# A graph layer with routed experts: sums added straight into the output, and the gate's logits taken from the node products

## What is computed

```python
xn = layernorm(x)
# graph part: gate of every edge, message, sum by target node, update
gate = sigmoid(silu(edge @ W1 + b1) @ W2 + b2)
aggr = segment_sum(gate * xn[src], dst)
upd  = silu(concat([xn, aggr]) @ U1 + c1) @ U2 + c2
# linear attention: kv = k^T v / N with layer-normed k and v; mix = (q @ kv) @ wo.T + bo
x = x + xn + upd + mix
# routed experts on the normed rows
xn2    = layernorm(x)
logits = xn2 @ gate_w + gate_b
top-2 softmax weights p; out = x + sum over the two experts of p * (silu(xn2 @ w1) * (xn2 @ w2)) @ w3
```

## Time and profile before

| | us |
|---|---|
| median of 3 runs | 1130.9 |
| lowest and highest | 1129.13, 1131.05 |
| the profiled execution, its own time | 1130.0 |
| the profiled execution, first to last instruction (span) | 1128.2 |
| mean granted TensorE clock, share of full speed | 0.957 |

### The profile page before, as it was taken

How to read it: one execution, slowest core, us unless ns; L and a number is a source line. 1 busy time by engine, 2 the same in 40 slices (tenths; PEclk the granted TensorE clock), 3 DMA queues, 4 the chain that set the end, 5 groups by cost and what they waited for, 6 DMA issues and landing times.

```text
span 1128.2 us, 23398 instructions
## 1 busy us (share of the span) xinstructions
PE 1033.9 (92%) x7884; PEld 978.0 (87%) x7884; DVE 889.9 (79%) x1411; ACT 686.0 (61%) x1055; POOL 746.6 (66%) x703
## 2 busy tenths in 40 slices
PE   4897999999999999999999999983499999999992
PEld 2466899999999999999999989983399999999991
DVE  7877998888999888888888843688487777777760
ACT  2562767766666666666666635652266777767760
POOL 5447877777777777777777756510267777767752
PEclk9998999999999999999999999985599999999996
DMA  7211444444444444444444401230678999888855
GB/s 241 77 53 42 135 146 143 143 141 141 143 143 142 140 141 141 143 143 141 141 141 143 125 26 56 85 104 1 178 215 226 230 235 226 237 233 235 227 119 137
DMA packets 118921, 165.25 MB, mean 146 GB/s; under 512 B 18625, under 2 KB 91382, under 8 KB 118774
## 3 DMA queue, kind: packets, MB, share of 16 engines
q1 hardware_dynamic: 87174, 95.14, 26.1%
q0 software_dynamic: 31104, 68.26, 25.3%
q10 hardware_dynamic: 560, 0.79, 0.2%
HBM read 145.62 MB, written 21.71 MB: 148 GB/s over the span
## 4 chain that ended last, share of the span: by engine, by line
POOL 39%; PE 37%; issue 13%; DVE 7%; DMA 2%; ACT 0%; POOLq 0%; DVEq 0%; ACTq 0%; SPq 0%
POOL big L590 19%; POOL hgx L590 19%; PE ps L1755 16%; PE ps L1767 8%; PE ps L1629 3%; PE ps L1502 2%; PE ps L1641 2%; PE ps L1654 2%; PE ps L1742 1%; PE ps L1668 1%; DVE st L961 1%; PE ps L1511 1%; PE ps L1512 1%; DMA hgx<-xn_rows,hgx 1%; PE ps L1495 1%
## 5 line engine op out<-in xcount | busy, mean ns | idle before, releaser
L1574 PE MATMUL ps<-fr 128*128 128x256 f32 x2352 | 306.9, 287 | 3.2 <-DVE fr L1023 3.2
L1574 PEld LDWEIGHTS ps<-fr 128*128 128x128 f32 x2352 | 289.4, 192 | 4.1 <-DVE fr L1023 4.0
L590 POOL DMA_INDIRECT big<-xn_rows,srcs x200 | 221.1, 1105 | 61.3 <-issue 61.3
L590 POOL DMA_INDIRECT hgx<-xn_rows,srcs x192 | 210.9, 1098 | 58.5 <-issue 58.5
L740 ACT ACTIVATE h1f<-ps,b 128x512 f32<-128x512 f32 x196 | 124.0, 684 | 165.5 <-PE ps L1528 164.3
L1585 PEld LDWEIGHTS ps<-oh,big 128*128 128x128 f32 x1568 | 189.8, 191 | 8.8 <-DVE big L1159 0.6
L1755 PE MATMUL ps<-fr 128*128 128x256 f32 x1536 | 192.0, 285 | 2.7 <-issue 1.4
L1755 PEld LDWEIGHTS ps<-fr 128*128 128x128 f32 x1536 | 188.6, 194 | 3.3 <-issue 1.8
L1585 PE MATMUL ps<-oh,big 128*128 128x96 f32 x1568 | 188.2, 273 | 0.5 <-DVE big L1168 0.5
L1023 DVE TENSOR_TENSOR fr<-h1f,fr 128x1024 fp32r<-128x1024 f32 x98 | 120.1, 1225 | 50.6 <-ACT fr L743 50.5
L661 POOL DMA_INDIRECT out_rows<-xnT,idx x64 | 115.4, 1803 | 35.6 <-POOL idx L657 24.2
(11 more groups left out here) (215 smaller groups left out, 1372.6 us busy)
## 6 DMA issues: line engine op xcount, KB each, us to landing
big<-in_w SPq DMA_DIRECT2D x128, 256.0 KB, 4.3
rbf<-in_rbf SPq DMA_DIRECT2D x98, 256.0 KB, 2.9
big<-in_w SPq DMA_DIRECT2D x32, 512.0 KB, 4.3
xn_rows<-xn SPq DMA_DIRECT2D x26, 128.0 KB, 2.4
big<-xn_rows,srcs POOLq DMA_INDIRECT x200, 3.1
out<-out_rows SPq DMA_DIRECT2D x1, 3125.0 KB, 11.9
xn_rows<-hgx SPq DMA_DIRECT2D x24, 128.0 KB, 2.2
hgx<-xn_rows,srcs POOLq DMA_INDIRECT x192, 3.1
```

The lines of the kernel that those rows point to most:

```text
L590: pool.indirect_dma_start(hg[i % HB][:, s, :], None, xn_d[:, :], bass.IndirectOffsetOnAxis(srcs[:, col:col + 1], 0))\
L1574: last = mm(ps[:, 2 + 4 * p + s // 2, (s % 2) * D:(s % 2 + 1) * D], h1s[p][a][:, c, s * P:(s + 1) * P], W2s[b][:, c, :], start=c == 0 and ...
```

## The change

It has these parts.

1. The scatter DMAs add into the output tensor itself; x is stored there (the last tile with its 53 rows). A row index above 3124 is skipped by the DMA (bounds_check, no error). acc_d, its spare rows and the closing copy are gone.
2. The logits. A logit is rstd times (x1 minus its mean) times the gate's weights, plus the bias. With the gate's weights centred over the features, the mean drops out, and what is left is linear in the sums that PE makes anyway. So the right-hand matrices U2 and M get 32 more columns (DG = 288): 16 for the part through the update and the mix, 16 for the part of x itself (std1, the old standard deviation, times xn). node_m and node_silu become 288 columns wide. Transposes, copy_xt2, gate_logits and copy_lg are gone.
3. Making those columns: new loads of wo, of U2 transposed and of the two biases (with gw at t = 2); on PE 2 products at t = 19, 10 at t = 23, 2 in mix_a1 and 4 at edge group 5, all of 16 columns in fp32; on VectorE centre_gate (t = 24), keep_gate (t = 27) and three more copies. GpSimd's first gather also waits for s_gt.
4. x1 has three instructions instead of one, and the first top of a batch two more.
5. Batches: CHUNKS (0, 6, 12, 20, 25); RCUT 12, 8, 5 tiles; TCUT 6, 6, 8, 5. The top steps move up to v = 3, 4, 6, 7, 10, 11, and low_marks(0), picked and ranks of batch 1, and low_marks(1) move behind the last count.
6. texp is made in two parts: the first two blocks' experts right after the counts, so that SP can load their weights then; the rest after the table. On SP the weights' loads of blocks 0 and 1 now stand ahead of the 8-byte DMA, which stands ahead of the wait for the second part.

The core of the diff:

```diff
+DG = D + 2 * NX
-CHUNKS = ((0, 6), (6, 12), (12, 16), (16, 20), (20, NT))
+CHUNKS = ((0, 6), (6, 12), (12, 20), (20, NT))
-RCUT = (0, 6, 12, NT)
+RCUT = (0, 12, 20, NT)
-TCUT = (0, 6, 12, 18, NT)
+TCUT = (0, 6, 12, 20, NT)
@@ SP
-                        sp.dma_start(acc_d[t0 * P:end * P, :].rearrange("(t p) d -> p t d", p=P), x[:, t0:end, :])\
+                        full = min(end, NT - 1)
+                        sp.dma_start(out_d[t0 * P:full * P, :].rearrange("(t p) d -> p t d", p=P), x[:, t0:full, :])\
                             .then_inc(s_acc, 16)
...
-            sp.wait_ge(s_wt, 1)
-            sp.dma_start(xn2_d[:, D:XW].rearrange("(t p) k -> p t k", p=P), wts).then_inc(s_wst, 16)
             sp.wait_ge(s_texp, 1)
...
             load_w(0, 0, True)
             load_w(1, 1, True)
+            sp.wait_ge(s_wt, 1)
+            sp.dma_start(xn2_d[:, D:XW].rearrange("(t p) k -> p t k", p=P), wts).then_inc(s_wst, 16)
+            sp.wait_ge(s_texp, 2)
...
-            sp.dma_start(out_d[:, :], acc_d[0:N, :]).then_inc(s_out, 16)
-            sp.wait_ge(s_out, 16)
+            sp.sem_inc(s_out, 1)
+            sp.wait_ge(s_out, 1)
@@ GpSimd
+            pool.wait_ge(s_gt, 2)
...
-                    pool.indirect_dma_start(acc_d[:, :], bass.IndirectOffsetOnAxis(idx[p][:, 2 + s:3 + s], 0),
-                                            ys[p][:, s, :], None, compute_op=ALU.add).then_inc(s_yst[p], 16)
+                    pool.indirect_dma_start(out_d[:, :], bass.IndirectOffsetOnAxis(idx[p][:, 2 + s:3 + s], 0),
+                                            ys[p][:, s, :], None, bounds_check=N - 1, oob_is_err=False,
+                                            compute_op=ALU.add).then_inc(s_yst[p], 16)
@@ VectorE
+            def centre_gate():
+                dve.wait_ge(s_gt, 1)
+                link(dve.scalar_tensor_tensor(gw[:, :, :], ps[:, 7, 16:16 + NX].unsqueeze(1).to_broadcast([P, DC, NX]),
+                                              -1.0 / D, gw[:, :, :], ALU.mult, ALU.add))
+                link(dve.tensor_tensor(cbT[:, :, 0], cbT[:, :, 0], cbT[:, :, 1], ALU.add))
+                link(dve.tensor_tensor(gcb[:, :, :], gw[:, :, :], cbT[:, :, 0:1].to_broadcast([P, DC, NX]), ALU.mult))
+                dve.sem_inc(s_gc, 1)
...
             def x1(v, q, n):
                 dve.wait_ge(s_uo, v + 3)
-                xr = x[:, 2 * v:2 * v + n, :]
-                dve.tensor_tensor(xr, ps[:, 2 + 2 * q:2 + 2 * q + n, 0:D], xr, ALU.add).then_inc(s_x1, 1)
+                of = ps[:, 2 + 2 * q:2 + 2 * q + n, :]
+                t = slice(2 * v, 2 * v + n)
+                link(dve.tensor_tensor(lg[:, t, :], of[:, :, D + NX:DG],
+                                       std1[:, t].unsqueeze(2).to_broadcast([P, n, NX]), ALU.mult))
+                dve.tensor_tensor(x[:, t, :], of[:, :, 0:D], x[:, t, :], ALU.add)
+                dve.tensor_tensor(lg[:, t, :], of[:, :, D:D + NX], lg[:, t, :], ALU.add).then_inc(s_x1, 1)
...
-            top2(12, 20)
-            picked(1)
-            ranks(1)
-            low_marks(1)
             top2(20, NT)
             count(2)
             link(dve.tensor_tensor(exw[:, :], tops[:, 1, :], tops[:, 0, :], ALU.subtract))
             dve.sem_inc(s_dif, 1)
+            low_marks(0)
...
+            experts(0, 2)
             places(0, 12)
             high_marks(0)
             high_marks(1)
-            picked(2)
-            ranks(2)
-            low_marks(2)
+            low_marks(1)
+            for r in (1, 2):
+                picked(r)
+                ranks(r)
             places(12, NT)
...
             high_marks(2)
+            low_marks(2)
+            high_marks(3)
+            low_marks(3)
+            dve.sem_inc(s_wsl, 2)
             dve.wait_ge(s_ex, 1)
@@ TensorE
+                if t == 19:
+                    pe.wait_ge(s_flag, 1)
+                    pe.wait_ge(s_gp, 64)
+                    for c in range(DC):
+                        last = mm(ps[:, 7, 16:16 + NX], ones[:, :], gw[:, c, :], start=c == 0, stop=c == DC - 1)
+                    last.then_inc(s_gt, 1)
+                if t == 23:
+                    pe.wait_ge(s_gc, 1)
+                    for at, of in ((32, U2L), (64, woL)):
+                        for m in range(DC):
+                            for c in range(DC):
+                                mm(ps[:, 7, at + m * NX:at + (m + 1) * NX], of[:, c, m * P:(m + 1) * P], gw[:, c, :],
+                                   start=c == 0, stop=c == DC - 1)
...
-                            last = mm(ps[:, 2 + 2 * q + h, 0:D], xns[q][a][:, k, h * P:(h + 1) * P],
+                            last = mm(ps[:, 2 + 2 * q + h, 0:DG], xns[q][a][:, k, h * P:(h + 1) * P],
                                       UMs[b][:, DC + k, :], start=k == 0 and (a, b) == PARTS[0], stop=False)
```

More of the change, by code:

```diff
@@ L159, in gps_layer @@
         M = wkv[:, :, 0:D]
+        MG = wkv[:, :, 0:DG]
+        gcb, g1 = (v_a[:, 64 + 32 * i:96 + 32 * i].rearrange("p (c n) -> p c n", c=DC) for i in range(2))
+        cg = v_b[:, 64:64 + NX]
+        std1 = v_c[:, 64:64 + NT]
+        cbT = v_c[:, 96:96 + 2 * DC].rearrange("p (c n) -> p c n", c=DC)
         big = sb("big", [P, NT * 2 * D])
@@ L214, in gps_layer @@
         oflat = [oh[i][:, :, :].rearrange("p s w -> p (s w)") for i in range(2)]
-        xt2 = [oflat[i % 2][:, i // 2 * D:(i // 2 + 1) * D].rearrange("p (c q) -> p c q", c=DC) for i in range(4)]
+        woL, U2L = (part(hgx, 1024 * i, DC, D) for i in range(2))
         khs = [oflat[i][:, 0:2 * (P + 2)].rearrange("p (j c) -> p j c", j=2) for i in range(2)]
@@ L413, in _ @@
                 (c1[:, :], c1_d),
[L414 removed]
+                (gb[:, :], row(gb_d, NX)),
             ]
@@ L860, in _ @@
             act.activation(hgx[:, 0:1], before[:, 0:1], ACT.Silu)
-            for c in range(NTC - 1):
+            for c in range(NTC):
                 act.wait_ge(s_eq, c + 1)
@@ L1088, in _ @@
                     dve.tensor_copy(flag[:, :], ps[:, 7, 0:1]).then_inc(s_flag, 1)
+                if t == NT - 1:
+                    centre_gate()
+                if t == NT + 2:
+                    keep_gate()
                 if t == NT + 3:
@@ L1352, in _, with experts @@
             link(dve.tensor_tensor(off, cend, c_e, ALU.subtract))
+            def experts(a, b):
+                shape = [P, b - a, NX]
+                link(dve.tensor_tensor(tcmp[:, a:b, :], cend.unsqueeze(1).to_broadcast(shape),
+                                       iota[:, a:b].unsqueeze(2).to_broadcast(shape), ALU.is_le))
+                link(dve.tensor_reduce(texp_f[:, a:b], tcmp[:, a:b, :], X, ALU.add))
+                link(dve.tensor_scalar(texp[:, a:b], texp_f[:, a:b], float(NX - 1), None, ALU.min))
+                dve.sem_inc(s_texp, 1)
             def places(a, b):
@@ L1418, in _ @@
             link(dve.tensor_copy(row, tab[:, :]))
-            dve.sem_inc(s_wsl, 2)
+            link(dve.tensor_scalar(lastp[:, :], cend[:, NX - 1:NX], -3.0, None, ALU.add))
+            link(dve.tensor_scalar(lastp[:, :], lastp[:, :], 1, None, ALU.arith_shift_right))
+            experts(2, CAPB)
             dve.sem_inc(s_hid, 2)
@@ L1537, in _ @@
                     sum_kv(t - KLAG, (t - KLAG) % 2, start=t == KLAG)
+                if t == 19:
[11 more added lines that the diff above has]
+                                   start=c == 0, stop=c == DC - 1)
+                    for c in range(DC):
+                        last = mm(ps[:, 7, 96:96 + NX], ones[:, :], gcb[:, c, :], start=c == 0, stop=c == DC - 1)
+                    last.then_inc(s_gt, 1)
                 if t == 16:
@@ L1553, in mix_a1 @@
                 for c in range(DC):
-                    last = mm(ps[:, 4, c * D:(c + 1) * D], kvt[:, c, :], woT[:, c, :], start=True, stop=True)
+                    mm(ps[:, 4, c * D:(c + 1) * D], kvt[:, c, :], woT[:, c, :], start=True, stop=True)
+                pe.wait_ge(s_gc, 2)
+                for c in range(DC):
+                    last = mm(ps[:, 7, 112 + c * NX:112 + (c + 1) * NX], kvt[:, c, :], g1[:, c, :], start=True, stop=True)
                 last.then_inc(s_mx, 1)
@@ L1586, in scatter @@
                                       oh[p][:, s, 0:w_n], start=s == 0, stop=s == ET - 1)
+                    if type(i) is int and i == 5:
+                        pe.wait_ge(s_mv, 3)
+                        for m in range(DC):
+                            for c in range(DC):
+                                last = mm(ps[:, 4 + p, 480 + m * NX:480 + (m + 1) * NX], wq[:, c, m * P:(m + 1) * P],
+                                          gcb[:, c, :], start=c == 0, stop=c == DC - 1)
                     last.then_inc(s_sc, 1)
@@ L1653, in node_silu @@
                         for a, b in PARTS:
[L1654 removed]
+                            last = mm(ps[:, 2 + 2 * q + h, 0:DG], sts[q][a][:, k, h * P:(h + 1) * P],
                                       UMs[b][:, k, :], start=False, stop=k == DC - 1 and (a, b) == PARTS[-1])
```

228 lines of the change are left out of this document (88 added, 140 removed).

## The result

The changed kernel takes 1119.8 us (median of 4 runs, 1118.2 to 1122.5), the one before 1131.0 beside it on the same chip: a ratio of 0.9907, with a 95% interval of 0.9883 to 0.9931. The gain is 11 us, where 18.8 were forecast. The profiled execution took 1118.8, with a span of 1116.9.

What follows compares the result with a forecast made beforehand. PE was taken to bound the node and expert stages, VectorE the routing, with no room in the edge stage. Closing copy -12.3, node -5.4, routing -5.9, first and edge +4.8 sum to -18.8 us: 1112 us, range 1104 to 1120.

Steps and rivals of the forecast that it cites:

- The closing copy: End of the kernel: without the copy the program ends at the last scatter's landing, 12.3 us less.
- The price of the columns: Node stage: 294 matmuls, each 32 columns wider, cost PE 14 ns apiece, 4.1 us more.
- the gate work: Node stage: transposes and gate products leave PE, 9.5 us less; net of the wider matmuls 5.4 less.
- What hides x1: Node stage: 2.88 us of U1 matmuls cover the longer x1; tightest at v = 9, done 2.2 us after release.
- Rival C: Less fast: VectorE late from v = 9, or first edge groups multiplying 4.8 into 10 to 12; 1119 to 1122, 8%.
- First and edge stages: Up to the end of the edges: new small products and VectorE steps add 4.8 us, bounds 3 and 7.
- the store's landing: First stage: new loads ahead of tile 3's store on SP's queue cost nothing, up to 1 us within the bounds.
- the half clock: First and edge stages: matmul records at half clock, 0.2 us each, at some places, within the upper bound of 7.
- Routing: Last full x1 to the counts 6.8 us less; counts to PE's start on the slots 0.9 more; together -5.9.
- Rival B: Routing, faster than forecast: the 8-byte DMA lands in 2 us, GpSimd starts 3.8 us earlier, 1108; 10%.
- Expert stage: PE's work and the scatters' issue time unchanged, skipped rows save traffic nobody waits for: 0.

Runs made afterwards that it cites:

- e6: The changed kernel with GpSimd's two-input work in the node stage cut to 8 columns per half, so its output differs: 1113.7 us.
- e4: The changed kernel with the routing weights computed right behind places(0, 12), so that the 8-byte DMA goes out earlier: 1114.0 us.
- e1: The kernel before with part 1 of the change alone (stores of x, row-limited scatters, no closing copy): 1118.9 us, ratio 0.9902.
- e16: The changed kernel with VectorE's small node-stage instructions spread over the pairs, nothing removed, third run of this kernel: 1114.1 us, ratio 0.9855.

## Why the prediction was too low

- **The closing copy, -12.3.** It is -11.3. The step took the copy's issue, at the landing of the last scatter, for the new end, 3.8 us behind that scatter's issue (1115.90 - 1112.08). The span runs 4.8 us past it, and not because of the landing, which comes after 2.7 us. What ends last is GpSimd's own closing instruction (DRAIN), at 1116.66. The kernel before has it at 1116.70, hidden under the copy.
- **The price of the columns, +4.1 for 294 matmuls, and the gate work, -9.5.** Right: the undisturbed period is 6.06 to 6.07 us, and e6 gives 79.3 for a stage of 79.1. (So close a hit has some luck in it: e6's first x1 came 12.6 us behind the first node products, against 11.8 before, and the rest was 0.6 shorter than 72.67 - 5.4.)
- **What hides x1.** This is the step that failed, and it holds 4.1 of the 7.6 us. The prediction priced VectorE's small instructions at 0.2 to 0.3 us, by rows of stretches in which GpSimd was idle, and looked for trouble at v = 9 alone, with 2.2 of 2.88 us used up. In the node stage the same instructions last up to 1.4 us beside GpSimd's. Rival C named VectorE coming late, with 8%, but not what makes it late; it began at v = 3. At v = 9 itself the next x1 starts 2.1 us late (8.13 us behind, at 749.47) instead of 1.1, and costs PE 0.3. The rows were there: in the trace of before the same chains were stretched too, to a mean of 538 ns for a 96-element compare that takes 258 undisturbed (e6) and 1208 in the changed kernel. There PE's gate work of 1.3 us in each of seven pairs lay over them, and PE did not wait. From x1 to x1 the kernel before needs 72.67 us and the changed one 72.09: taking the gate work from PE gave 0.6, and e6 gets 5.4 more. The gain went into a wait for VectorE that only appears once PE's own work is gone.
- **First and edge stages, +4.8.** The terms hold, one by one: 0.36 at t = 19 for 0.4; products 2.26 and wait 0.44 for 2.5; mix_a1 0.4 (118.52 to 118.89) for 0.5; group 5 0.84 (162.92 to 163.76) for 0.8. Only keep_gate's 0.6 doesn't show: in e4 the way from the last projection to the first gate products is 0.2 longer than before. In e4 those come 3.2 us later than before; with 0.4 and 0.8 in the edge stage that is 4.4. What the sum put at nothing, or within its bounds, is the store's landing ("nothing, up to 1 us") and the half clock at the projection (3.29 for 1.88). They make the profiled execution 2.4 longer than the forecast, and other executions of the same stage don't have them, or have less.
- **Routing, -6.8 and +0.9.** Right in both, and in the mechanism: e4 took the wait away and got 4.3 us back, its price. The second figure is helped by luck: counts to gather took 32.4 us for 31.1, since the DMA landed in 6.9 instead of 5.9, and gather to PE 4.2 for 5.3, since the first gathers landed in 2.7 to 2.8 instead of 3.9. The two misses cancel. Rival B (a landing of 2 us) falls: 6.9 here, 5.9 before, and 9.7 in e4, where the experts' weights load beside it. The fit that the prediction cited of the Trainium skill, "DMA: Bandwidth & Descriptors", section "Anatomy of one DMA", gave 2.1 us. The page states it for DMAs that GpSimd issues, and these three readings of one that SP issues, with 8 bytes a row, are three to five times as long.
- **Expert stage, 0.** Right; e1 shows it for the row limit by itself.

The Trainium skill has the rule that would have caught the failed step: "GPSIMD Engine Reference", section "Specifications", says that GpSimd shares its SBUF interfaces with VectorE and that it contends with VectorE's instructions that have two SBUF inputs or run in a 2-port mode. The trace agrees, with 0.17 against 1.22 to 1.29 us for the same instruction, and with x1, which has only one input in SBUF (on-chip memory), the other in PSUM (where PE writes its sums): it takes 0.69 us with GpSimd busy or not, its last instruction 0.18.

## What to carry to other kernels

Before work is taken off the engine that bounds a stage, measure what the next engine needs for the same stage, in the rows of that stage and beside its neighbours: here durations from a quiet stretch didn't hold beside GpSimd. Chains of small linked VectorE instructions belonged into the gaps of GpSimd's two-input work, behind the instruction that another engine waits for (3.4 us). And when a DMA joins the conditions of a start, see whether its data can be made earlier: here moving three small instructions gave 4.3 us.

## What the runs showed of the hardware

- VectorE is not slowed by a share beside GpSimd, but held. In the changed kernel, between the first full x1 and the last, 18 small VectorE instructions with two inputs in on-chip memory start while a GpSimd TENSOR_TENSOR of 1.3 us runs; all 18 end 0.02 to 0.15 us behind the end of one of GpSimd's, whether they have 6 or 128 elements a partition. GpSimd's own keep their 1.3 us. TENSOR_REDUCE (0.25 us) and the batch-norm statistics (0.42) are not held. A one-input TENSOR_SCALAR on f32 was, too (1.08 instead of 0.17, e16).
- 32 more columns, 256 to 288, cost 13 ns a matmul: twelve in 686.20 - 684.60 = 1.60 us, 0.133 each, against 0.120.
- A scatter-add DMA of 128 rows with a row limit lasts as long as one without: 1578 ns against 1616 in the median.
- GpSimd's closing DRAIN ends 3.02 to 3.08 us behind the end of its last scatter DMA's issue in all 18 traces. Without a copy behind it, it ends the program, though in the changed kernel the data had landed 1.8 us before.
- One and the same stretch of PE work ran at either clock level in different executions: the last projection took 3.29 us at a granted clock of 0.50 and 1.96 at 1.00, behind a wait of 0.44 and 0.45 us. Without the wait and the small products ahead of it, it was 1.88 in all eight executions; with them, longer than 1.96 in four of ten. What decides between the ten stays open.
